# Attention probabilities turned by VectorE and DMA instead of TensorE, values kept by token, in a six-layer local-attention stream

## Chip, cores and metric

One core of a Trainium2 chip runs the whole program. The metric is the device time in microseconds (us); the median of three runs of the kernel before is 1961.72 us (1958.45 to 1962.31).

## What is computed

The input is 2 sequences of 1024 tokens of width 128. A first phase (an RWKV-style recurrent layer, about the first 300 us, not touched by the change) is followed by six layers of local attention and a gated feed-forward. The part that the change touches, for each layer, with 16 heads of width 64 and windows of 32 tokens:

```python
qkv = x @ Wqkv;  q, k, v = split(qkv)            # 16 heads of 64
q, k = l2norm(q) * qs, l2norm(k) * ksc           # then rotary position, scaled
bk2, bv2 = look(bk), look(bv)                    # keys and values of this window of 32 and the one before
sim = einsum('bhwie,bhwje->bhwij', bq, bk2) * 8.0
attn = softmax(where(mask, -max, sim), -1)       # 32 queries x 64 keys, per window and head
out = einsum('bhwij,bhwje->bhwie', attn, bv2)
x = x + out @ Wo
x = x + (a * gelu(gate)) @ W2 + b2               # a, gate = layernorm(x) @ W1 + b1
```

## The kernel before

The stream phase treats 96 blocks of 128 tokens (16 blocks a layer, six layers) as one software pipeline. `stream(turn)` calls, for each engine, its own function `turn` once a block number n; inside it `at(lag, stage)` runs a stage for block n - lag, and `pair(lag, stage)` one for a pair of blocks, only in odd or only in even turns. The order within an engine is the order of the lines of its `turn`; nothing reorders it. Engines meet through counting semaphores: `X.after(n)` is the count once stage X has finished block n.

A block's way, with its lag: project q, k (four PSUM banks, `project_qk`) and v (`project_v`); VectorE multiplies by the rotary tables (`rotate`, three instructions a bank), ScalarE squares for the norms (`square`), VectorE sums them (`norms`); GpSimd adds the turned half (`add_turned`) and scales by the inverse norms (`unit`), all at lag 0 and 1. At lag 2 TensorE turns k and q (`turn_k`, `turn_q`), ScalarE reads them out, TensorE makes the scores (`scores`), VectorE takes the peaks and subtracts them, ScalarE takes the exponent (`exponent`), VectorE sums and inverts (`totals`), GpSimd scales (`unit_probs`). At lag 3 TensorE turns the probabilities (`turn_p`, eight 128x128 transposes into banks 6 and 7), ScalarE copies them out (`read_p`) into `p_T`, and TensorE makes the outputs (`outputs`, 64 small products of 64 rows by 64 columns by 32). These need the values of two windows as rows, which SyncE's queue places with 16 DMAs of 64 KB a block (`place_v`, into `v_win`). Lags 4 to 6 hold, for pairs of blocks: output projection (`project_o`), residual (`add_attention`), centring product (`centres`), variance, and the feed-forward.

Two turns make a pair: in the even turn TensorE has in addition the variances and the first gate products, in the odd turn the rest of the feed-forward, the output projection and, last, `centres`. I call the even turn **A** and the odd one **B**; a pair as measured here runs from one `centres` to the next. GpSimd's turn begins with `table_gains`, which makes the rotary tables that `rotate` of the same block waits for.

## Time and profile before

| what | value |
|---|---|
| median of 3 runs | 1961.72 us |
| profiled execution: its own time | 1961.85 us |
| its span in the trace | 1960.1 us |
| mean granted TensorE clock | 0.968 |
| busy, whole span: PE / DVE / ACT / POOL | 1809.8 / 1488.0 / 1241.2 / 1234.4 us |
| PE matmuls of `turn_p` | 768 (8 a block) |
| DMAs `v_win<-v_tok` | 1536 of 64.0 KB (16 a block) |

PE is TensorE's matmuls, PEld its weight loads, DVE VectorE, ACT ScalarE, POOL GpSimd, SP the queue of SyncE. Instructions that read at once as "x4" are merged; their durations overlap with the next row's start, because ends are modelled, so distances from start to start are what adds up. TensorE's records come in two for each fp32 product and in one for each transpose.

### The profile page before, as it was taken

What the parts mean: (1) busy time and instruction counts of PE and PEld (TensorE: products, weight loads), DVE (VectorE), ACT (ScalarE), POOL (GpSimd) and SP (SyncE); (2) the same over time, 40 slices, a digit from 0 to 9 for tenths busy, and PEclk for the clock granted to TensorE, in tenths of its full rate; (3) what the DMA queues carried; (4) which work ended last, traced back from release to release, by engine and by line L of the source; (5) the groups of instructions that cost most, each with busy time, mean ns of one, the idle gap of its engine ahead of it and who ended that gap; (6) DMA issues with size and microseconds to landing.
All of it is one profiled execution on the core that took longest, in us unless ns stands there. A gap on an engine that the chain in (4) does not pass through costs nothing.

```text
span 1960.1 us, 75595 instructions
## 1 busy us (share of the span) xinstructions
PE 1809.8 (92%) x31926; PEld 1253.5 (64%) x31926; DVE 1488.0 (76%) x2822; ACT 1241.2 (63%) x2413; POOL 1234.4 (63%) x789
## 2 busy tenths in 40 slices
PE   7477876999999999999999999999999999999995
PEld 2144453667667667777777767677767776666773
DVE  6699947878777778787878777787878787777763
ACT  6523214577676767676767676767676767677662
POOL 3466733766666666666666666666666666666650
PEclk9799967999999999999999999999999999999996
DMA  4444002222222242222423222422224222222220
GB/s 100 123 53 56 17 3 83 63 67 67 67 66 62 68 117 71 64 72 60 122 70 73 63 67 61 125 61 72 62 70 121 70 64 69 65 67 67 66 69 22
DMA packets 89777, 137.48 MB, mean 70 GB/s; under 512 B 27168, under 2 KB 32736, under 8 KB 88416
## 3 DMA queue, kind: packets, MB, share of 16 engines
q1 hardware_dynamic: 89440, 132.66, 28.2%
q8 instruction: 252, 4.13, 0.9%
q14 instruction: 85, 0.70, 0.1%
HBM read 29.79 MB, written 2.10 MB: 16 GB/s over the span
## 4 chain that ended last, share of the span: by engine, by line
PE 49%; DVE 14%; issue 8%; POOL 6%; ACT 6%; DVEq 0%; SPq 0%; ACTq 0%; POOLq 0%; DMA 0%
PE bank L1435 8%; PE bank L1342 8%; PE bank L1417 7%; PE bank L1355 7%; PE bank L1390 5%; DVE turnedhalf L1762 5%; PE bank L1347 5%; PE bank L1452 4%; PE bank L1476 3%; POOL probs L1304 3%; DVE qk L1758 2%; POOL qk L1280 2%; DVE rnorm L1768 2%; ACT q_T L1604 1%; DVE probs L1781 1%
## 5 line engine op out<-in xcount | busy, mean ns | idle before, releaser
L1286 POOL TENSOR_TENSOR qk<-qk,rnorm 128x1024 f32<-128x1024 f32 x192 | 361.4, 1903 | 366.0 <-ACT rnorm L1592 275.4
L1280 POOL TENSOR_TENSOR qk<-qk,turnedhalf 128x1024 f32<-128x1024 f32 x192 | 454.7, 2368 | 138.8 <-DVE turnedhalf L1762 138.8
L1758 DVE TENSOR_TENSOR qk<-bank,gains 128x512 f32<-128x512 f32 x384 | 262.8, 684 | 222.0 <-ACT squares L1582 207.8
L1342 PE MATMUL bank<-wqkv,x 128*128 128x512 f32 x768 | 378.1, 596 | 4.7 <-DVE v_tok L1738 2.9
L1582 ACT ACTIVATE squares<-bank 128x512 f32<-128x512 f32 x384 | 232.6, 606 | 153.4 <-PE bank L1342 150.6
L1762 DVE TENSOR_TENSOR turnedhalf<-bank,gains 128x256 f32<-128x256 f32 x768 | 286.3, 414 | 0.0
L1629 ACT ACTIVATE o_T<-bank 128x512 f32<-128x512 f32 x192 | 104.2, 598 | 229.5 <-PE bank L1417 229.5
L1768 DVE TENSOR_REDUCE rnorm<-squares 128x16 f32<-128x1024 f32 x192 | 230.8, 1202 | 2.8
L1417 PEld LDWEIGHTS bank<-p_T,v_win 64*64 64x64 f32 x12288 | 189.9, 135 | 60.2 <-issue 57.6
L1355 PEld LDWEIGHTS bank<-st_ident,qk 128*128 128x128 f32 x1536 | 178.6, 142 | 57.1 <-issue 50.9
L1347 PE MATMUL bank<-wqkv,x 128*128 128x512 f32 x384 | 202.5, 609 | 7.0 <-DVE turnedhalf L1762 6.9
L1417 PE MATMUL bank<-p_T,v_win 64*64 64x32 f32 x12288 | 201.6, 220 | 8.0 <-issue 5.6
L1355 PE MATMUL bank<-st_ident,qk 128*128 128x128 f32 x1536 | 192.7, 274 | 0.0
L1304 POOL TENSOR_TENSOR probs<-probs,total 128x1024 f32<-128x1024 f32 x96 | 182.9, 1905 | 13.5 <-DVE total L1790 13.5
L1342 PEld LDWEIGHTS bank<-wqkv,x 128*128 128x128 f32 x768 | 138.6, 191 | 68.4 <-issue 55.1
L1435 PE MATMUL bank<-o_T,wo 128*128 128x256 f32 x768 | 173.8, 379 | 0.0
L1435 PEld LDWEIGHTS bank<-o_T,wo 128*128 128x128 f32 x768 | 145.8, 190 | 39.4 <-issue 22.0
L1452 PE MATMUL bank<-xn_T,w 128*128 128x256 f32 (+1 forms) x576 | 163.5, 393 | 7.7 <-ACT gate_T L1655 1.5
L1390 PE MATMUL bank<-k_T,q_T 64*32 64x64 f32 x12288 | 156.6, 225 | 12.8 <-issue 11.3
L1390 PEld LDWEIGHTS bank<-k_T,q_T 64*32 64x32 f32 x12288 | 136.6, 105 | 37.7 <-issue 34.0
L1808 DVE SCALAR_TENSOR_TENSOR ff_T<-bank,b,gate_T 128x256 f32<-128x256 f32 x144 | 64.7, 477 | 117.2 <-PE bank L1452 117.2
L1622 ACT ACTIVATE p_T<-bank 128x512 f32<-128x512 f32 x192 | 104.3, 594 | 75.5 <-PE bank L1355 74.4
(197 smaller groups left out, 2946.9 us busy)
## 6 DMA issues: line engine op xcount, KB each, us to landing
v_win<-v_tok SPq DMA_DIRECT2D x1536, 64.0 KB
wqkv<-in_wqkv SPq DMA_DIRECT2D x6, 1536.0 KB
v_rep_sb<-v_by_step SPq DMA_DIRECT2D x32, 128.0 KB
v_rep<-v_by_step SPq DMA_DIRECT2D x32, 128.0 KB
wo<-in_wo SPq DMA_DIRECT2D x6, 512.0 KB
w<-in_w SPq DMA_DIRECT2D x6, 341.0 KB
w<-in_w SPq DMA_DIRECT2D x6, 192.0 KB
xT_sb<-in_xT SPq DMA_DIRECT2D x1, 1024.0 KB, 4.9
```

Of the source, the lines that this page charges most:

```text
L1280: nc.gpsimd.tensor_tensor(out=qk[n % 2][:, half], in0=qk[n % 2][:, half], in1=turnedhalf[:, half], op=ALU.add).then_inc(rot_added.sem, 1)
L1286: nc.gpsimd.tensor_tensor(out=by_head(qk[u][:, half]), in0=by_head(qk[u][:, half]), in1=rnorm[u][:, AH * i:AH * (i + 1)].unsqueeze(2).to_b ...
L1342: nc.tensor.matmul(QK_BANKS[i][:, :], shifted_tokens(x, n, P), layer_cols(wqkv, n, 3 * INNER, 512 * i, 512), start=True, stop=True).then_i ...
L1347: nc.tensor.matmul(V_BANKS[i][:, :], shifted_tokens(x, n, P), layer_cols(wqkv, n, 3 * INNER, 2 * INNER + 512 * i, 512), start=True, stop=T ...
L1355: mm = nc.tensor.transpose(outs[i // 4][:, P * (i % 4):P * (i % 4 + 1)], source[:, P * i:P * (i + 1)], ident[:, :])
L1390: mm = nc.tensor.matmul(s_banks(n)[p][at:at + WINDOW, 2 * WINDOW * a_:2 * WINDOW * (a_ + 1)], q_T[rows, a_, at:at + WINDOW], k_T[rows, a_, ...
L1417: mm = nc.tensor.matmul(s_banks(n)[p][DH * side:DH * (side + 1), P * q + at:P * q + at + WINDOW], v_win[n % 2][rows, w, DH * a_:DH * (a_ + ...
L1435: mm = nc.tensor.matmul(ff_bank(m)[:, 0:PT], layer_cols(wo, n, INNER, C * i, C), o_T[:, i, :], start=(i == 0), stop=(i == PAIRS - 1))
L1452: mm = nc.tensor.matmul(ff_bank(m)[0:size, PT * j:PT * (j + 1)], layer_cols(w1, PAIR * m, 2 * FF, at + f0, size), xn_T[:, :], start=True, ...
L1758: nc.vector.tensor_tensor(by_head(qk[u][:, cols]), src, cos.to_broadcast([P, 8, DH]), ALU.mult).then_inc(rotated.sem, 1)
L1762: nc.vector.tensor_tensor(by_head(turnedhalf[:, cols])[:, :, to], src[:, :, frm], sin[:, :, to].to_broadcast([P, 8, half]), ALU.mult).then ...
L1768: nc.vector.reduce_sum(rnorm[n % 2][:, AH * h:AH * (h + 1)], by_head(squares[:, INNER * h:INNER * (h + 1)]), AX).then_inc(ss_made.sem, 1)
```

## The change

1. Probabilities: TensorE's eight transposes and ScalarE's two copies a block go. One VectorE instruction turns all 32x32 pieces of a block's probabilities into `p_blocks` (new `turn_p`, first in VectorE's turn), and eight DMAs of 32 partitions by 2 KB bring them to the rows where `outputs` reads them (new `place_p`, into two buffers `p_T`). In SyncE's queue the probabilities of block n - 2 (LAG_P = 2) go ahead of the values of block n.
2. Values: ScalarE writes them by token as they come (`read_v`, four buffers instead of three). `outputs` takes half its windows straight from `v_tok`, and the others from `v_shift`, the same shifted by 32 tokens, which two DMAs a block fill in place of 16. The same 64 products a block now run in another order: two column halves of the same rows, then two of the other rows.
3. Outputs are written to the scores' banks as before, with rows and columns laid out by window pair; `read_o` and the host's layout of Wo follow. `turn_k` waits only for the last block's copies.
4. Order: `totals` ahead of the last `rotate` on VectorE, `unit_probs` ahead of the second `add_turned` on GpSimd, `project_qk(2)` right behind the scores on TensorE. The end of the program is ordered anew.

```diff
-    v_win = two("v_win", (P, WINDOWS, INNER // 2))
-    probs, p_T = two("probs", (P, PAIRS, 2, DH)), sb("p_T", (P, PAIRS, P))
+    v_shift = two("v_shift", (P, INNER))
+    probs, p_T = two("probs", (P, PAIRS, 2, DH)), two("p_T", (P, 2, AH, WINDOW))
+    p_blocks = sb("p_blocks", (P, 2, AH, WINDOW))
...
         def place_v(n):
             sp.wait_ge(v_read.sem, v_read.after(n))
             sp.wait_ge(o_product.sem, o_product.after(n - 2))
             sp.wait_ge(v_placed.sem, v_placed.after(n - 1))
-            for p in range(2):
-                cols = slice(p * INNER // 2, (p + 1) * INNER // 2)
-                for w in range(WINDOWS):
-                    own, before = slice(WINDOW * w, WINDOW * (w + 1)), slice(WINDOW * (w - 1), WINDOW * w)
-                    sp.dma_start(v_win[u][DH * p + WINDOW:DH * (p + 1), w, :], tok[own, cols]).then_inc(v_placed.sem, 16)
-                    src = tok[before, cols] if w else last[P - WINDOW:P, cols]
-                    sp.dma_start(v_win[u][DH * p:DH * p + WINDOW, w, :], src).then_inc(v_placed.sem, 16)
+            sp.dma_start(v_shift[u][WINDOW:P, :], tok[0:P - WINDOW, :]).then_inc(v_placed.sem, 16)
+            sp.dma_start(v_shift[u][0:WINDOW, :], last[P - WINDOW:P, :]).then_inc(v_placed.sem, 16)
+        def place_p(n):
+            sp.wait_ge(p_turned.sem, p_turned.after(n))
+            sp.wait_ge(o_product.sem, o_product.after(n - 2))
+            sp.wait_ge(p_placed.sem, p_placed.after(n - 1))
+            for w in range(WINDOWS):
+                for half in range(2):
+                    row = DH * (w // 2) + WINDOW * half
+                    sp.dma_start(p_T[n % 2][row:row + WINDOW, w % 2, :, :], p_blocks[WINDOW * w:WINDOW * (w + 1), half, :, :]).then_inc(p_placed.sem, 16)
+        def place(n):
+            if n >= LAG_P:
+                place_p(n - LAG_P)
+            place_v(n)
...
         def outputs(n, q):
             if q == 0:
-                pe.wait_ge(pT_made.sem, pT_made.after(n))
...
+                pe.wait_ge(v_read.sem, v_read.after(n))
                 pe.wait_ge(v_placed.sem, v_placed.after(n))
+                pe.wait_ge(p_placed.sem, p_placed.after(n))
-            for w in range(WINDOWS):
-                for side in range(2):
-                    for p in range(2):
+            for a_ in (2 * q, 2 * q + 1):
+                for turn_ in range(2):
+                    v = v_tok[n % V_SLOTS] if turn_ else v_shift[n % 2]
+                    for g in range(2):
+                        for p in range(2):
+                            rows, head = slice(DH * g, DH * (g + 1)), 2 * a_ + p
+                            at = DH * a_ + WINDOW * turn_
+                            mm = nc.tensor.matmul(o_banks(n)[g][DH * p:DH * (p + 1), at:at + WINDOW], v[rows, DH * head:DH * (head + 1)],
+                                                  p_T[n % 2][rows, turn_, head, :], start=True, stop=True, skip_group_check=True)
...
+        def turn_p(n):
+            dve.wait_ge(p_normed.sem, p_normed.after(n))
+            dve.wait_ge(p_placed.sem, p_placed.after(n - 1))
+            nc.vector.transpose(p_blocks[:, :, :, :], probs[n % 2][:, :, :, :].rearrange("t a p (g k) -> t g (a p) k", k=WINDOW)).then_inc(p_turned.sem, 1)
```

On VectorE, in turn A and up to the start of turn B, there stood before (L1758 and L1762 are `rotate`, L1788 and L1790 `totals`, L1768 `norms`, L1808 `gated_full`):

```order
L1768 TENSOR_REDUCE rnorm<-squares 128x16
L1758 TENSOR_TENSOR qk<-bank,gains 128x512
L1762 TENSOR_TENSOR turnedhalf<-bank,gains 128x8x32 x2
L1758 TENSOR_TENSOR qk<-bank,gains 128x512
L1762 TENSOR_TENSOR turnedhalf<-bank,gains 128x8x32 x2
L1788 TENSOR_REDUCE total<-probs 128x16
L1790 RECIPROCAL total<-total 128x16
L1768 TENSOR_REDUCE rnorm<-squares 128x16
L1808 SCALAR_TENSOR_TENSOR ff_T<-bank,b,gate_T 128x256 x2
```

and at the same place there now stands (the line numbers of the changed kernel: L1764 and L1768 `rotate`, L1794 and L1796 `totals`, L1774 `norms`, L1802 the new `turn_p`, L1820 `gated_full`):

```order
L1774 TENSOR_REDUCE rnorm<-squares 128x16
L1764 TENSOR_TENSOR qk<-bank,gains 128x512
L1768 TENSOR_TENSOR turnedhalf<-bank,gains 128x8x32 x2
L1794 TENSOR_REDUCE total<-probs 128x16
L1796 RECIPROCAL total<-total 128x16
L1764 TENSOR_TENSOR qk<-bank,gains 128x512
L1768 TENSOR_TENSOR turnedhalf<-bank,gains 128x8x32 x2
L1774 TENSOR_REDUCE rnorm<-squares 128x16
L1802 STREAM_TRANSPOSE p_blocks<-probs 128x1024
L1820 SCALAR_TENSOR_TENSOR ff_T<-bank,b,gate_T 128x256 x2
```

The sums moved ahead of the last rotation, and the block transpose came in behind the norms' sum.

On GpSimd, from one `table_gains` (L1273) to the next, there stood before (L1286 `unit`, L1280 `add_turned`, L1304 `unit_probs`, L1298 or L1296 the halo of k):

```order
L1273 TENSOR_TENSOR gains<-tables,qk_gain 128x256
L1286 TENSOR_TENSOR qk<-qk,rnorm 128x1024 x2
L1280 TENSOR_TENSOR qk<-qk,turnedhalf 128x1024 x2
L1304 TENSOR_TENSOR probs<-probs,total 128x1024
L1273 TENSOR_TENSOR gains<-tables,qk_gain 128x256
```

and now stands (L1296 is now `table_gains`, L1309 `unit`, L1303 `add_turned`, L1327 `unit_probs`, L1319 the halo):

```order
L1296 TENSOR_TENSOR gains<-tables,qk_gain 128x256
L1309 TENSOR_TENSOR qk<-qk,rnorm 128x1024 x2
L1303 TENSOR_TENSOR qk<-qk,turnedhalf 128x1024
L1327 TENSOR_TENSOR probs<-probs,total 128x1024
L1303 TENSOR_TENSOR qk<-qk,turnedhalf 128x1024
```

The scaling of the probabilities moved between the two additions; all three still lie ahead of the next block's tables.

## Rows read from the trace of the kernel before

**Rows 1.** Busy time by engine in one steady pair (instruction counts, granted clock, DMA share, GB/s).

```profile
1023.35:1055.83 32.48, 32.37 (x627) 23.19 (x628) 25.73 (x49) 23.34 (x45) 22.39 (x14) 1.00 0.28 67
```

**Rows 2.** PE timeline, same pair: start us, us, engine line op, tiles, count.

```profile
1023.20 0.70 PE L1442 MATMUL bank<-xm,centring 128*128 128x256 f32 x2
...
1034.89 2.07 PE L1417 MATMUL bank<-p_T,v_win 64*64 64x32 f32 x128
1036.89 1.13 PE L1347 MATMUL bank<-wqkv,x 128*128 128x512 f32 x2
...
1042.88 0.66 PE L1452 MATMUL bank<-xn_T,w 128*85 128x256 f32 x2
...
1045.33 1.09 PE L1355 MATMUL bank<-st_ident,probs 128*128 128x128 f32 x8
1046.26 1.46 PE L1476 MATMUL bank<-ff_T,w 128*128 128x256 f32 x6
...
1055.68 0.70 PE L1442 MATMUL bank<-xm,centring 128*128 128x256 f32 x2
```

**Rows 3.** DVE timeline, same pair: brackets give idle time before and releaser.

```profile
1028.37 0.69 DVE L1758 TENSOR_TENSOR qk<-bank,gains 128x512 f32<-128x512 f32 x1 [4.34 <-ACT squares L1582]
...
1036.00 0.68 DVE L1758 TENSOR_TENSOR qk<-bank,gains 128x512 f32<-128x512 f32 x1
...
1037.27 1.21 DVE L1788 TENSOR_REDUCE total<-probs 128x16 f32<-128x1024 f32 x1
1038.51 0.25 DVE L1790 RECIPROCAL total<-total 128x16 f32<-128x16 f32 x1
1038.68 1.16 DVE L1768 TENSOR_REDUCE rnorm<-squares 128x16 f32<-128x1024 f32 x1
1041.95 0.88 DVE L1808 SCALAR_TENSOR_TENSOR ff_T<-bank,b,gate_T 128x256 f32<-128x256 f32 x2 [2.11 <-PE bank L1452]
1042.75 0.68 DVE L1758 TENSOR_TENSOR qk<-bank,gains 128x512 f32<-128x512 f32 x1
...
1054.43 0.82 DVE L1795 TENSOR_TENSOR xm<-bank,x 64x256 f32<-64x256 f32 x2
```

**Rows 4.** POOL timeline, same pair.

```profile
1037.43 2.37 POOL L1280 TENSOR_TENSOR qk<-qk,turnedhalf 128x1024 f32<-128x1024 f32 x1 [0.81 <-DVE turnedhalf L1762]
1039.76 1.90 POOL L1304 TENSOR_TENSOR probs<-probs,total 128x1024 f32<-128x1024 f32 x1
1041.62 0.74 POOL L1273 TENSOR_TENSOR gains<-tables,qk_gain 128x256 f32<-128x256 f32 x1
```

**Rows 5.** First and last centring product of the steady stretch, PE timeline (46 pairs).

```profile
393.55 1.22 PE L1442 MATMUL bank<-xm,centring 128*128 128x256 f32 x2 [1.60 <-DVE xm L1795]
...
1883.55 0.70 PE L1442 MATMUL bank<-xm,centring 128*128 128x256 f32 x2
```

**Rows 6.** PE timeline of a longer pair, 661.5 to 695.3.

```profile
676.13 0.32 PE L1417 MATMUL bank<-p_T,v_win 64*64 64x32 f32 x7 [1.02 <-issue]
```

**Rows 7.** DVE groups by line and shape, 0 to 320 us: the only block transpose.

```profile
L725 DVE STREAM_TRANSPOSE v_rep_sb<-decay 128x256 f32<-128x256 f32 x8 | 3.0, 419 | 0.0
```

**Rows 8.** Chain of waits, 1000 to 1060: start us, us, what.

```profile
1047.72 1.72 PE bank L1342 x4
...
1050.30 3.45 PE bank L1435 x16
1053.75 2.04 PE bank L1417 x128
```

**Rows 9.** SP timeline: the last placement of a block.

```profile
1046.84 0.59 SPq L1231 DMA_DIRECT2D v_win<-v_tok  x1
```

**Rows 10.** DMA busy tenths, 40 slices, 1045 to 1050 us.

```profile
DMA  0485105952010049510496104691000000000000
```

**Rows 11.** DMA rate, 40 slices, 969 to 989 us, after a layer's weights are issued.

```profile
GB/s 74 127 131 221 74 270 418 393 467 393 418 418 320 393 380 319 229 286 312 264 404 206 205 206 252 209 119 82 37 152 115 70 98 33 0 0 0 0 0 0
```

**Rows 12.** PE timeline of the end: outputs of the last block.

```profile
1913.65 2.07 PE L1417 MATMUL bank<-p_T,v_win 64*64 64x32 f32 x128 [2.20 <-ACT p_T L1622]
```

98 lines of the change are left out of this document (44 added, 54 removed).

## Prediction

> **What bounds the kernel now.** I first read the busy time of one steady pair. TensorE is busy 32.37 of 32.48 us, VectorE 25.73, ScalarE 23.34, GpSimd 22.39, at full granted clock [rows 1]. So TensorE sets the pace of a pair: from one centring product to the next, 1055.68 - 1023.20 = 32.48 us [rows 2]. Second, the timelines of the other engines over the same pair, for how far behind that pace they are. VectorE has two gaps a pair: 4.34 us ahead of turn A's first rotation, until ScalarE's squares come, and 2.11 us ahead of turn B's gated product, until TensorE has made it [rows 3]. They look like ample room, but a loop runs beside TensorE that is almost as long: first rotation of A at 1028.37; its last ends when GpSimd's addition starts, 1037.43; GpSimd then works without a gap, addition, probabilities, tables, until 1041.62 + 0.74 = 1042.36; turn B's first rotation, which waits for those tables, starts at 1042.75; the residual ends at 1054.43 + 0.82 = 1055.25; the centring product starts at 1055.68 [rows 2 to 4]. Of the 32.48 us this loop has 0.39 + 0.43 us of slack. That is what the change can win before something else is the bound.
>
> Third, all pairs: 46 centring products from 393.55 to 1883.55, so 45 pairs of 33.11 us on average [rows 5]. The 0.63 us above 32.48, 28 us in all, are mostly stops like the one of [rows 6]: TensorE waits 1.02 us in the middle of a train of small products, for nothing that the trace shows.
>
> **The change, part by part.** The sum is made per pair, then times 45, plus the ends.
>
> *TensorE.* Turn_p takes 1046.26 - 1045.33 = 0.93 us from start to start [rows 2], twice a pair: -1.86 us of TensorE, so its own work is 30.62 us. ScalarE's two copies a block go too; ScalarE is not short of time, and nothing in the loop waits for them.
>
> *Outputs.* 64 products of the same shape. Their order goes from alternating row halves to two column halves of the same rows at a time. The trace has 2.04 us for the 128 records [rows 8], 16 ns each, and no train in the new order. Lower bound: no change. Upper bound: twice as slow, 4 us, if two products on the same rows no longer overlap. I take no change: the weights of a full-array product seem to cost nothing although they go to the rows that are in use. Four records of 512 columns take 1.72 us, 430 ns each; sixteen of 256 columns take 3.45 us, 216 ns each [rows 8], so the time follows the columns and no fixed part for a weight load is left.
>
> The Trainium skill says the contrary of this reading: TensorE: Matmul & The Clock Gate, The mechanism, has weight loads overlap running products only where the row group differs. By it the new order, with pairs on the same rows, would be slower than the old. The trace of before agrees with it in the small products only so far that they alternate rows; in the full-array products it disagrees. What it would do here is the second rival.
>
> *VectorE.* One block transpose of 128x1024 a block. The trace has one of 128x256, 419 ns [rows 7]; four times that is 1.68 us, and as a single sweep like the sum of 128x1024 it is 1.21 us [rows 3]. In A it follows the norms' sum, which ends at 1038.68 + 1.16 = 1039.84. Even with 1.68 it ends at 1041.52, ahead of the 1041.95 at which the gated product can start. In B it falls into the gap of 4.34 us. I cost it at nothing; it would start to cost beyond 1.8 us, since the two gated products (0.80 us from 1041.95 to 1042.75) must then be done by the 1042.50 at which the tables come, below.
>
> *The reordering, on the loop.* The last rotation used to start at 1036.00 in A. Now the sums start there and their inverse is ready 1038.51 + 0.25 - 1037.27 = 1.49 us later, 1037.49. The handover to GpSimd, 0.08 us, gives 1037.57. Then GpSimd has the same three instructions as before in another order, 1.86 + 2.33 + 0.74 us (start to start) [rows 4], until 1042.50, and turn B's first rotation follows at 1042.56. Before, it started at 1042.75, held by the gated products; those are now 0.9 us earlier with TensorE. So this half gains 0.19 us.
>
> *Turn B.* From its first rotation to the end of the residual VectorE has 1055.25 - 1042.75 = 12.50 us without a wait on TensorE [rows 3], with the same instructions in another order. The residual now ends at 1055.06, and the centring product starts at 1055.12 in place of 1055.68. TensorE, 1.86 us of work shorter, is there before and waits more than 1 us. From the centring product to A's first rotation it is 5.17 us (1023.20 to 1028.37) as before, through TensorE's v and k products and ScalarE. So a pair takes 32.48 - 0.56 = 31.92 us, and 45 pairs save 25 us.
>
> *The stops.* In B TensorE now has 1.3 us to spare before it holds the loop (1.86 less the 0.56 gained), in A about half a us. A stop of 1 us costs its full length now; half of them should disappear in that room: -14 us, between 0 and -28.
>
> *SyncE's queue.* A block's probabilities need eight issues of 1047.43 - 1046.84 = 0.59 us [rows 9], 0.63 us apart, 5.05 us, and the last placement's packets are gone by 1048.4, 1.0 us after its issue [rows 9, 10]. In A, the tighter turn, counted from the centring product: the norms' sum ends at +1.1, the transpose at +2.8 at the latest, the issues at +7.8, the data at +8.9. The outputs start at 1034.89 - 1023.20 - 0.93 = +10.76 [rows 2]. So 1.8 us are left, and the transfers are hidden. The values' two DMAs are issued when the outputs of the block two before are done, ahead of the probabilities of the next, and do not queue behind them. If that cover goes, TensorE waits in `outputs`, and the k and q of the next turn, the gated product and the loop wait behind it.
>
> *Layer loads.* Four times, 2.7 MB of weights are issued directly behind the values, and now directly ahead of a block's probabilities. The transfer of those weights runs at some 400 GB/s and has died down after about 15 us, the v placements among them [rows 11]; 2.7 MB at 370 GB/s are 7.3 us. Probabilities queued behind them land at about +10 to +12 against +10.76. I take +1 us each, +4, between 0 and +12.
>
> *The end.* The last block's outputs start at 1913.65, released by ScalarE's copy [rows 12]. There the path of the probabilities lies open: 1.2 to 1.7 + 5.05 + 1.0 us in place of 0.93 and about 1.1 us. That is +5 us, less what TensorE no longer does there: +4, between 0 and +8.
>
> Sum: -25 - 14 + 4 + 4 = -31 us against the profiled execution's 1961.85 us, which stands 0.1 us from the median of the runs. Forecast: **1931 us**.
>
> **Rivals.** (a) *TensorE stays the bound*, since the loop is shorter than I read it: the pair falls to 30.6 us, 45 x 1.86 = 84 us less, 1878 us. For it: TensorE has nearly no gap now. Against: the GpSimd chain has none either, from 1037.43 to 1042.36.
>
> (b) *Outputs in the new order are slow.* Place: every `outputs`. At 4 us instead of 2.04, TensorE's pair is 30.62 + 4 = 34.6 us, 2.1 us more than now, 45 x 2.1 = +95 us and the ends: 2060 us, slower. It decides against the change from 2.04 + 0.93 = 3.0 us per block. At 2.7 us it costs almost nothing, in the room that TensorE has won. The skill's rule, above, points here.
>
> (c) *Probabilities come late in every turn.* If an issue takes 0.9 instead of 0.63 us, or a landing 3 us instead of 1, `outputs` of A starts some 0.5 to 1 us late; the gain of 0.56 is used up once the lateness goes beyond about 2.4 us. Then about 1965 us, slower or the same.
>
> (d) *Nothing changes*: the transpose takes over 2.4 us, or the loop grows elsewhere by what it gains, 1958 to 1964 us.
>
> **How the numbers follow.** My forecast (faster by 5 to 57 us, 1905 to 1957): 0.66. (a) 0.07, (b) 0.10, (c) 0.08, (d) 0.09. The forecast's own range comes from the bounds: -25 - 28 = -53, or 1909, and -25 + 12 + 8 = -5, or 1957. For 8 in 10 I take in (d) and half of (c): 1900 to 1965. A measurement here tells about 0.2%, 4 us, from no change. Faster 0.73 (forecast and (a)), same 0.10, slower 0.17 ((b) and most of (c)).
>
> **What would show it.** In the profile after: pairs of 31.9 us between centring products; TensorE busy about 30.6 us in each, and waiting over 1 us at the centring product for VectorE's residual; turn B's first rotation released by GpSimd's tables; the block transpose between 1.2 and 1.7 us, in both turns without a product waiting on it; a train of outputs of 2.0 us; TensorE waiting for no DMA in `outputs` but at four layer starts and at the end. I am wrong if the train of outputs is much longer, if its start is released by a DMA in ordinary turns, or if the pair is 30.6 us.

## The result, and the profile after

The changed kernel takes 1952.92 us (median of 20 runs, 1944.96 to 1959.65) where the kernel before takes 1963.18 us (20 runs on the same chips, 1955.27 to 1968.52). The ratio is 0.9949, with a 95% interval of 0.9937 to 0.9962: faster by 0.5%, about 10 us. I had forecast 31 us. The direction is right and the time lies inside the range, but the forecast is three times too large, and the reason for that is most of what follows. That the time lies inside the range is in part luck: one term missed its own bounds by far, and others, larger than forecast the other way, made up for some of it.

The page of the profiled execution after, its busy times and the DMA queue of instructions:

```profile
span 1954.8 us, 73483 instructions
...
PE 1766.6 (90%) x31158; PEld 1188.3 (61%) x31158; DVE 1598.5 (82%) x2918; ACT 1138.5 (58%) x2221; POOL 1233.5 (63%) x789
...
q8 instruction: 246, 4.03, 0.9%
```

TensorE is 43 us less busy, VectorE 111 us more (a block transpose of 1.24 us a block is 119 us of it). The span is only 5.3 us shorter: this execution took 1956.77 us, 4 us more than the median of its kernel, and the one profiled before 1.3 us less than the median of its own. What follows takes these two spans apart, not the 10 us of the medians.

One steady pair, its busy times (the stretch that answers to [rows 1]), and the two centring products that bound it, with the outputs of its second turn between them:

```profile
1022.02:1053.80 31.78, 31.33 (x611) 21.61 (x611) 28.00 (x51) 21.16 (x42) 22.35 (x14) 1.00 0.26 69
```

```profile
1021.96 0.70 PE L1462 MATMUL bank<-xm,centring 128*128 128x256 f32 x2 [0.26 <-DVE xm L1807]
...
1051.44 0.32 PE L1438 MATMUL bank<-p_T,v_shift 64*64 64x32 f32 x8
...
1053.76 0.70 PE L1462 MATMUL bank<-xm,centring 128*128 128x256 f32 x2 [0.26 <-DVE xm L1807]
```

A pair takes 1053.76 - 1021.96 = 31.80 us, where it took 32.48 [rows 2]; most pairs of the stretch take 31.78 to 31.80, and I use 31.79. The bracket is the new thing: at 40 of the 46 centring products TensorE now waits for VectorE's residual, where it did at one of 46 before. VectorE in the pair before that one:

```profile
1002.99 1.22 DVE L1794 TENSOR_REDUCE total<-probs 128x16 f32<-128x1024 f32 x1
...
1006.74 1.24 DVE L1802 STREAM_TRANSPOSE p_blocks<-probs 128x1024 f32<-128x1024 f32 x1
1008.20 0.88 DVE L1820 SCALAR_TENSOR_TENSOR ff_T<-bank,b,gate_T 128x256 f32<-128x256 f32 x2 [0.22 <-PE bank L1472]
1009.57 0.69 DVE L1764 TENSOR_TENSOR qk<-bank,gains 128x512 f32<-128x512 f32 x1 [0.50 <-issue]
...
1021.04 0.87 DVE L1807 TENSOR_TENSOR xm<-bank,x 64x256 f32<-64x256 f32 x2
...
1027.13 0.69 DVE L1764 TENSOR_TENSOR qk<-bank,gains 128x512 f32<-128x512 f32 x1 [2.82 <-ACT squares L1598]
```

And GpSimd in the same stretch, which answers to [rows 4]:

```profile
1004.57 1.90 POOL L1327 TENSOR_TENSOR probs<-probs,total 128x1024 f32<-128x1024 f32 x1 [0.97 <-DVE total L1796]
1006.43 2.36 POOL L1303 TENSOR_TENSOR qk<-qk,turnedhalf 128x1024 f32<-128x1024 f32 x1
1008.75 0.73 POOL L1296 TENSOR_TENSOR gains<-tables,qk_gain 128x256 f32<-128x256 f32 x1
```

This is the loop as the prediction has it: the sums, then GpSimd's probabilities, addition and tables without a gap until 1009.48, then turn B's first rotation at 1009.57, for which VectorE stood 0.50 us. The row names no releaser, but GpSimd's tables, for which this rotation waits, end 0.09 us before it.

All pairs together, first and last centring product, for [rows 5]:

```profile
397.61 0.70 PE L1462 MATMUL bank<-xm,centring 128*128 128x256 f32 x2 [1.60 <-DVE xm L1807]
...
1868.11 0.70 PE L1462 MATMUL bank<-xm,centring 128*128 128x256 f32 x2
```

45 pairs in 1470.5 us, where they took 1490.0: 19.5 us less. With the pair at 31.79 and 32.48 us, the difference of the two spans is made up of five terms:

| term | before | after | difference |
|---|---|---|---|
| 45 pairs at the steady length | 1461.6 | 1430.6 | -31.0 us |
| excess of the four pairs at layer loads | 4.2 | 31.5 | +27.3 |
| excess of the other pairs (stops) | 24.2 | 8.4 | -15.8 |
| start to first centring product | 393.6 | 397.6 | +4.1 |
| last of these products to the end | 76.6 | 86.7 | +10.1 |
| span | 1960.1 | 1954.8 | -5.3 |

So most of the gain was given back at four places, and more of it at the two ends. Pairs at the loads took 40.57, 38.34, 41.69 and 38.05 us (34.00, 32.68, 34.82 and 32.57 before). SyncE's queue at the first of them, and TensorE there (all rows of `outputs` but the first are left out):

```profile
689.25 0.53 SPq L1213 DMA_DIRECT2D wqkv<-in_wqkv  x1
689.82 0.44 SPq L1213 DMA_DIRECT2D wo<-in_wo  x1
690.30 1.03 SPq L1213 DMA_DIRECT2D w<-in_w  x2
691.38 1.30 SPq L1214 DMA_DIRECT2D qk_gain<-in_qk_gain  x1
692.80 5.00 SPq L1243 DMA_DIRECT2D p_T<-p_blocks  x8
```

```profile
697.68 1.02 PE L1370 MATMUL bank<-wqkv,x 128*128 128x512 f32 x2
704.25 0.44 PE L1438 MATMUL bank<-p_T,v_shift 64*64 64x32 f32 x8 [5.55 <-DMA p_T<-p_blocks]
...
707.82 2.07 PE L1370 MATMUL bank<-wqkv,x 128*128 128x512 f32 x2
```

The placements of the probabilities are issued behind 2.7 MB of weights, and `outputs` waits 5.55 us for them (7.24 us at the third load). Then the loss goes on: the train of 128 records takes 707.8 - 704.2 = 3.6 us, not 2.04, since the granted clock stands at 0.50, the lower of TensorE's two levels (1.2 and 2.4 GHz), from 704.2 to 708.0, as the windows show:

```profile
697.00:702.00 5.00, 1.70 (x4) 0.40 (x3) 4.96 (x9) 3.66 (x5) 4.20 (x3) 1.00 0.87 232
704.20:708.00 3.80, 3.75 (x129) 3.71 (x130) 1.39 (x2) 0.00 (x0) 2.90 (x2) 0.50 0.02 4
708.00:716.00 8.00, 8.00 (x28) 5.10 (x28) 0.81 (x3) 6.13 (x11) 0.00 (x0) 0.72 0.49 131
```

(After the times: busy of PE, PEld, DVE, ACT and POOL, then granted clock, DMA share and GB/s.) TensorE stood idle from 698.7 to 704.2. The granted clock was still 1.00 until 702.0 and is 0.50 from 702.5 on, so it fell within the wait, and it stayed there until 712.

At the second and fourth load it looks otherwise. TensorE stops in the middle of the scores, and nothing in the trace releases it:

```profile
957.55 1.48 PE L1413 MATMUL bank<-k_T,q_T 64*32 64x64 f32 x120
962.61 0.44 PE L1413 MATMUL bank<-k_T,q_T 64*32 64x64 f32 x8 [3.59 <-issue]
```

`outputs`, which comes behind, does not wait for the probabilities there. The stop is not the whole cost of 6.5 us here either: the granted clock is 1.00 from 959.0 to 961.6 and 0.50 behind it.

```profile
961.80:968.40 6.60, 5.79 (x17) 3.20 (x18) 4.87 (x8) 0.60 (x1) 3.43 (x2) 0.50 0.60 156
```

### The profile page after: what moved, and what is told of

The parts are those of the page before. It is cut to its first block, busy times and chain, and to the rows that moved or that the text cites. A ratio compares the mean times of both kernels' runs of the same rounds, so it can differ in the third digit from the quotient of the medians.

```text
span 1954.8 us, 73483 instructions
## 1 busy us (share of the span) xinstructions
PE 1766.6 (90%) x31158; PEld 1188.3 (61%) x31158; DVE 1598.5 (82%) x2918; ACT 1138.5 (58%) x2221; POOL 1233.5 (63%) x789
## 4 chain that ended last, share of the span: by engine, by line
PE 31%; DVE 22%; issue 9%; POOL 9%; DMA 6%; ACT 3%; SPq 2%; DVEq 0%; ACTq 0%; POOLq 0%
PE bank L1455 7%; DVE turnedhalf L1768 6%; DMA v_shift<-v_tok 5%; POOL qk L1303 5%; PE bank L1438 5%; PE bank L1365 5%; PE bank L1413 4%; DVE qk L1764 3%; DVE total L1794 3%; DVE rnorm L1774 3%; PE bank L1496 3%; PE bank L1370 3%; POOL probs L1327 2%; PE bank L1472 2%; DVE probs L1787 2%
## 5 line engine op out<-in xcount | busy, mean ns | idle before, releaser
L1309 POOL TENSOR_TENSOR qk<-qk,rnorm 128x1024 f32<-128x1024 f32 x192 | 361.0, 1901 | 316.4 <-ACT rnorm L1608 310.9
L1303 POOL TENSOR_TENSOR qk<-qk,turnedhalf 128x1024 f32<-128x1024 f32 x192 | 454.4, 2367 | 7.5 <-DVE turnedhalf L1768 7.5
L1365 PE MATMUL bank<-wqkv,x 128*128 128x512 f32 x768 | 406.5, 614 | 8.0 <-issue 3.0
L1764 DVE TENSOR_TENSOR qk<-bank,gains 128x512 f32<-128x512 f32 x384 | 258.1, 672 | 159.1 <-ACT squares L1598 138.6
L1327 POOL TENSOR_TENSOR probs<-probs,total 128x1024 f32<-128x1024 f32 x96 | 182.7, 1903 | 180.6 <-DVE total L1796 180.6
L1768 DVE TENSOR_TENSOR turnedhalf<-bank,gains 128x256 f32<-128x256 f32 x768 | 286.2, 415 | 0.0
L1774 DVE TENSOR_REDUCE rnorm<-squares 128x16 f32<-128x1024 f32 x192 | 233.2, 1214 | 2.8
L1438 PEld LDWEIGHTS bank<-p_T,v_shift 64*64 64x64 f32 x6144 | 168.9, 138 | 75.1 <-issue 46.2
L1438 PE MATMUL bank<-p_T,v_shift 64*64 64x32 f32 x6144 | 194.1, 223 | 22.3 <-DMA p_T<-p_blocks 17.1
L1370 PE MATMUL bank<-wqkv,x 128*128 128x512 f32 x384 | 205.0, 616 | 4.7 <-DVE turnedhalf L1768 4.2
L1438 PE MATMUL bank<-p_T,v_tok 64*64 64x32 f32 x6144 | 192.8, 222 | 3.7 <-issue 3.7
L1413 PE MATMUL bank<-k_T,q_T 64*32 64x64 f32 x12288 | 164.0, 225 | 16.9 <-issue 15.7
L1438 PEld LDWEIGHTS bank<-p_T,v_tok 64*64 64x64 f32 x6144 | 170.0, 138 | 4.4 <-issue 4.4
L1413 PEld LDWEIGHTS bank<-k_T,q_T 64*32 64x32 f32 x12288 | 141.6, 105 | 45.4 <-issue 38.8
L1472 PEld LDWEIGHTS bank<-xn_T,w 128*128 128x128 f32 (+1 forms) x576 | 99.2, 184 | 101.2 <-DVE ff_T L1820 45.9
```

The source lines that it names most:

```text
L1303: nc.gpsimd.tensor_tensor(out=qk[n % 2][:, half], in0=qk[n % 2][:, half], in1=turnedhalf[:, half], op=ALU.add).then_inc(rot_added.sem, 1)
L1309: nc.gpsimd.tensor_tensor(out=by_head(qk[u][:, half]), in0=by_head(qk[u][:, half]), in1=rnorm[u][:, AH * i:AH * (i + 1)].unsqueeze(2).to_b ...
L1365: nc.tensor.matmul(QK_BANKS[i][:, :], shifted_tokens(x, n, P), layer_cols(wqkv, n, 3 * INNER, 512 * i, 512), start=True, stop=True).then_i ...
L1370: nc.tensor.matmul(V_BANKS[i][:, :], shifted_tokens(x, n, P), layer_cols(wqkv, n, 3 * INNER, 2 * INNER + 512 * i, 512), start=True, stop=T ...
L1413: mm = nc.tensor.matmul(s_banks(n)[p][at:at + WINDOW, 2 * WINDOW * a_:2 * WINDOW * (a_ + 1)], q_T[rows, a_, at:at + WINDOW], k_T[rows, a_, ...
L1438: mm = nc.tensor.matmul(o_banks(n)[g][DH * p:DH * (p + 1), at:at + WINDOW], v[rows, DH * head:DH * (head + 1)], p_T[n % 2][rows, turn_, he ...
```

## Experiments

Ratios are to the kernel before, timed beside each; the changed kernel has 0.9949. Each experiment starts from the changed kernel unless the text says otherwise.

### e1: the load behind the placements

```diff
+            place_p(layer * BLOCKS + EARLY - LAG_P)
...
             load_layer(sp, layer + 1, (layer + 1) % 2)
-            for n in range(EARLY, BLOCKS):
+            place_v(layer * BLOCKS + EARLY)
+            for n in range(EARLY + 1, BLOCKS):
                 place(layer * BLOCKS + n)
```

> The changed kernel with one edit: at each of the four layer loads inside the stream, SyncE issues the eight placements of the waiting block's turned probabilities before the five transfers of the next layer's weights, not behind them. In the changed kernel the four pairs at the loads take 40.6, 38.3, 41.7 and 38.1 us against 31.8 us for the others, +31.5 us in all. Theory A (the probabilities queue behind the weights, and outputs waits for them): the four pairs fall to at most 34 us each, so 22 to 31 us come back and the median is about 1926 us (1921 to 1932). Theory B (the weights fill the DMA engines, and TensorE stops for its own instructions whatever the order of the issues is): only the two loads at which outputs waited for the probabilities gain, about half of it, 1936 to 1943 us; the two loads at which TensorE stopped for 3.5 to 3.8 us inside the scores keep their stops.

Measured: 1931.73 us, ratio 0.982 (0.9797 to 0.9843), 25 us faster than the changed kernel by the ratios. SyncE now issues the placements at 687.65, the weights at 692.70:

```profile
687.65 4.95 SPq L1243 DMA_DIRECT2D p_T<-p_blocks  x8
692.70 1.10 SPq L1213 DMA_DIRECT2D wqkv<-in_wqkv  x1
```

The pairs at the first and third load are now 31.77 and 31.78 us, so all of their excess is gone. The other two hardly changed, 38.18 and 37.76 us; the second one:

```profile
940.21 0.70 PE L1464 MATMUL bank<-xm,centring 128*128 128x256 f32 x2 [0.26 <-DVE xm L1809]
...
956.86 0.31 PE L1440 MATMUL bank<-p_T,v_tok 64*64 64x32 f32 x2 [2.92 <-issue]
...
978.39 0.70 PE L1464 MATMUL bank<-xm,centring 128*128 128x256 f32 x2 [0.25 <-DVE xm L1809]
```

So in places theory B is right: two loads gain and two keep stops. This pair has two, 0.90 and 2.92 us; the first ends at 948.23, ahead of the weights, which are issued at 948.72. Its time, 1936 to 1943 us, was too high, because the two waits for the probabilities were worth 19 us and not half of 31.5, and some further microseconds came from elsewhere.

### e4: the load in parts

```diff
+    LOAD_PARTS = [("wqkv", c, c + 512) for c in range(0, 3 * INNER, 512)] + ...
...
-            load_layer(sp, layer + 1, (layer + 1) % 2)
             for n in range(EARLY, BLOCKS):
                 place(layer * BLOCKS + n)
+                i = n - EARLY
+                if i == 0:
+                    load_gain(sp, layer + 1, (layer + 1) % 2)
+                for part in range(2 * i, min(2 * i + 2, len(LOAD_PARTS))):
+                    load_part(sp, layer + 1, (layer + 1) % 2, part)
```

> The changed kernel with one edit: each of the four layer loads inside the stream is cut into eleven parts of at most 256 KB, of which SyncE issues two behind the placements of each block, from the block on at which the whole load was issued before. Theory A (order behind the weights): the probabilities never wait for more than two parts, so the loads' +31.5 us fall to a few us: about 1926 us. Theory B (the DMA engines are full during a load, and TensorE's own instructions come late): as the engines are never full for longer than 1 to 2 us, its stops of 3.5 to 3.8 us go as well, and this kernel is faster than the one that only moves the load behind the probabilities: 1920 to 1930 us here, against 1936 to 1943 there. If both come out alike within 3 us, TensorE's stops at the loads cost nothing of their own. Against both: each part costs SyncE about 0.63 us of issuing, eleven instead of four, which could make the placements later by 1.3 us a block; then the blocks of the load lose up to 6 x 1.3 = 8 us a layer.

Measured: 1923.09 us, ratio 0.9782 (0.976 to 0.9804). The pair at the second load is 972.12 - 939.82 = 32.30 us:

```profile
939.82 0.70 PE L1477 MATMUL bank<-xm,centring 128*128 128x256 f32 x2 [0.25 <-DVE xm L1822]
...
972.12 0.70 PE L1477 MATMUL bank<-xm,centring 128*128 128x256 f32 x2 [0.25 <-DVE xm L1822]
```

No pair at a load is longer than 32.6 us, and no train of the steady stretch is stopped for more than 1.5 us. The four loads are now all but free, and against e1 8.6 us came back (the intervals of the ratios just touch; timed together, all five runs of e4 are faster than all four of e1). So the long stops came with the whole load in the engines at once, and the twelve issues in place of five cost SyncE nothing that shows in the time.

### e2: the order of sums and probabilities undone

```diff
-            at(2, totals)
             at(0, rotate, 3)
+            at(2, totals)
...
-            at(2, unit_probs)
             at(0, add_turned, 1)
+            at(2, unit_probs)
```

> The changed kernel with the two moves in order undone: on VectorE the sums of the exponentials stand behind the last rotation of the bank again, and on GpSimd the product that makes unit probabilities stands behind both additions of the rotation. The instructions are the same. Theory A (a loop through VectorE and GpSimd sets the pair: rotation, sums, unit probabilities, additions, next rotation, residual, centring product): the unit probabilities and with them the placements come later, and the loop is longer by what was moved out of it; pair 33.0 us in place of 31.8, +54 us, about 2005 us. Theory B (TensorE sets the pair with its stops and trains, and the others have room): within 0.3% of the changed kernel, 1948 to 1958 us.

Measured: 2003.88 us, ratio 1.0194 (1.0167 to 1.0221). The pair is 1075.28 - 1042.48 = 32.80 us, 1.0 us more than in the changed kernel, and the order on GpSimd shows why: its addition waits for the last rotation, and the tables end at 1028.85, after which turn B begins.

```profile
1023.92 2.37 POOL L1303 TENSOR_TENSOR qk<-qk,turnedhalf 128x1024 f32<-128x1024 f32 x1 [0.81 <-DVE turnedhalf L1768]
1026.24 1.90 POOL L1327 TENSOR_TENSOR probs<-probs,total 128x1024 f32<-128x1024 f32 x1
1028.11 0.74 POOL L1296 TENSOR_TENSOR gains<-tables,qk_gain 128x256 f32<-128x256 f32 x1
```

Theory A holds, with 1.0 us where I had 1.2. It also says what the rest of the change is worth without these two moves: the kernel is 1.9% slower than before. VectorE's block transpose then waits 1.85 us for GpSimd's probabilities and holds turn B's rotations, which start at 1030.10, 1.25 us after the tables.

### e3 and b1: the tables earlier, in both kernels

```diff
         def turn(at, pair):
             at(2, halo)
-            at(0, table_gains)
             at(1, unit, 0)
             at(1, unit, 1)
+            at(-1, table_gains)
...
+        table_gains(0)
```

> The changed kernel with GpSimd's product for the tables of the next block made right behind the two unit products of the block before, a turn's slack ahead of where it stands now (behind the unit probabilities and additions). The instructions are the same. Theory A (GpSimd's additions, tables and unit probabilities lie in the loop that sets the pair, and VectorE's second rotation of a pair waits for the tables): the loop is shorter by the part of the tables' 0.8 us that it now spends in it, pair 31.3 in place of 31.8 us, -22 us: 1931 us (1926 to 1940). Theory B (TensorE or VectorE alone sets the pair): no change, 1948 to 1958 us.

> The kernel before with GpSimd's product for the tables moved as in the run with early tables, nothing else. In the changed kernel this move took 0.35 us off each pair. The prediction held that the kernel before is bound by TensorE (pair 32.48 us), and the loop through VectorE and GpSimd bounds only the changed one. Theory A (so it is): no change, ratio 0.998 to 1.002, about 1965 us. Theory B (the loop already bounded the kernel before): pair 0.3 to 0.4 us shorter, 14 to 18 us, ratio 0.991 to 0.993.

Measured: e3 1943.54 us, ratio 0.988 (0.9858 to 0.9902); pair 1045.82 - 1014.39 = 31.43 us, 0.36 less. The tables are made at 1025.44, the two additions and the probabilities stand alone in the loop:

```profile
1025.44 0.74 POOL L1296 TENSOR_TENSOR gains<-tables,qk_gain 128x256 f32<-128x256 f32 x1
...
1028.77 1.91 POOL L1327 TENSOR_TENSOR probs<-probs,total 128x1024 f32<-128x1024 f32 x1 [0.27 <-DVE total L1797]
1030.64 2.36 POOL L1303 TENSOR_TENSOR qk<-qk,turnedhalf 128x1024 f32<-128x1024 f32 x1
```

The same edit in the kernel before (b1) gives 1962.9 us, ratio 0.9988 (0.9973 to 1.0004): nothing. So the first reading of the prediction holds on both sides. TensorE bounds the kernel before, and the loop through VectorE and GpSimd bounds the changed one. Of the 0.74 us of the tables only 0.36 us is gained, so something else holds the pair at 31.43 us. What it is I did not take apart; e8, below, shows that VectorE's order is still part of it.

### b2: the kernel before with its loads in parts

The edit of e4, in the kernel before.

> The kernel before with its layer loads cut into the same eleven parts, two behind the placements of each block. In its trace the pairs at the loads are no longer than the others. Theory A (the kernel before has nothing to gain there, so that the cost of the loads is one that the change brought): ratio 0.998 to 1.002, about 1965 us. Theory B (its stops of TensorE, 28 us over the stream, come partly from the loads): 0.995 to 0.998. Against both: its sixteen transfers a block take SyncE 10 us of the 16, and two more issues a block might make it late: then over 1.002.

Measured: 1962.25 us, ratio 0.9983 (0.9972 to 0.9995). That is 3 us, about the 4.2 us of excess that its pairs at the loads had, where the same edit brings 33 us in the changed kernel. The loads' cost came with the change, all but a small part. Two things are new. The probabilities stand behind the weights in SyncE's queue, which accounts for the first and third load (e1). And the weights are issued 1.1 to 1.6 us behind the centring product, in e1 7.4 to 8.5 us, where it was 10.9 to 11.6 us before, so they meet other work of TensorE. Whether that is why the kernel before has no long stop at its second and fourth load, no run tells.

### e7: the order of the outputs

```diff
-                for turn_ in range(2):
-                    v = v_tok[n % V_SLOTS] if turn_ else v_shift[n % 2]
-                    for g in range(2):
+                for g in range(2):
+                    for turn_ in range(2):
+                        v = v_tok[n % V_SLOTS] if turn_ else v_shift[n % 2]
```

> The changed kernel with its outputs' products in another order within each of the four parts of a train: the half of TensorE's rows (64 of 128) on which a product works changes every fourth product, where it changes every second in the changed kernel and every product in the kernel before. Theory A (the train's time is one issue of 16 ns per record, whatever the halves): 128 records in 2.04 us again, the same span as the changed kernel to 0.3%. Theory B, after the rule of the Trainium skill, page TensorE: Matmul & The Clock Gate, section The mechanism (a weight load hides behind running products only where its rows differ from theirs): three of four loads now stand in the same half, and the train takes longer than 2.04 us, by at least 10%.

Measured: one run, 1949.6 us, span 1947.7. The chain of waits has a steady train of the changed kernel, and below it one of e7:

```profile
1019.71 2.04 PE bank L1438 x128
```

```profile
1014.40 2.08 PE bank L1438 x128
```

The train of e7 is 2% longer, where theory B wants at least 10%, and the four pairs at the loads keep their excess (38.5 to 39.7 us), so the span, of a single run, is that of the changed kernel to 0.4%. With the row half changing every product (before, [rows 8]), every second (changed) or every fourth (e7), the train takes 2.04, 2.04 and 2.08 us. The rule of the Trainium skill, page TensorE: Matmul & The Clock Gate, section The mechanism, that a weight load overlaps running products only where its row group differs, is not seen in these trains of fp32 products of 32 columns; the measurement decides.

### e10: one and a half loads

e1, and behind each load one more transfer of 1.5 MB of weights into a spare buffer in DRAM that nothing reads.

> The kernel in which the layer load is issued behind the placements of the probabilities, with one more transfer behind each of the four loads: the 1.5 MB of the query, key and value weights are copied a second time, into a spare buffer in DRAM that nothing reads. No computation changes. Theory A (TensorE stops when its own instructions are fetched while the DMA engines are full; in the changed kernel a fetch of 16 KB came every 5 to 7 us, and at the second load none between 952.6 and 961.8 us while TensorE stood from 959.0 to 962.6): with the engines full for some 5 us longer at each load, stops of 2 us and more come at all four loads, not at two, and the time rises by 6 to 25 us over 1929 us. Theory B (the stops come from something at these places in the program and not from the transfers): they stay as they are at the second and fourth load, none come at the others, and the time stays within 3 us.

Measured: 1934.61 us, ratio 0.9847 (0.9817 to 0.9877), 5 us more than e1 by the ratios, within the two intervals. A stop came at the third load, whose pair is 35.04 us (31.78 in e1):

```profile
1227.28 0.48 PE L1503 MATMUL bank<-ff_T,w 85*128 85x256 f32 x1 [2.07 <-issue]
```

None came at the first, and the other two kept theirs, shorter than in e1 (36.19 and 36.48 us). Theory A expected all four and theory B none. This does not settle it: one more load has a stop, and the time did not move beyond the noise.

### e12: TensorE's instructions shifted

e1, and ahead of the stream 128 waits in place of one:

```diff
-        pe.wait_ge(masks_made.sem, 3)
+        for _ in range(128):
+            pe.wait_ge(masks_made.sem, 3)
```

> The kernel in which the layer load is issued behind the placements, with 128 further instructions ahead of TensorE's stream (waits on a semaphore that has long been set). In the trace the transfers of the instruction queue with 16 KB each come once for every 256 instructions of TensorE (246 of them for 31158 products, as many weight loads and 839 semaphore instructions), and against the pairs their times repeat every 5.5 pairs or so; as a layer has 8 pairs, the second and fourth load meet them half a cycle away from the first and third. Theory A (a fetch that falls into the time of a load comes late, and TensorE stops when it has run through what it has): 128 instructions are half a cycle, so the stops change places: the pairs at the first and third load now take 36 to 39 us, those at the second and fourth 31.8 to 33 us, and the time stays within 6 us of 1929. Theory B (the stops come from the place in the layer's program or from the load alone): second and fourth load take 38 us again, first and third 31.8.

Measured: 1930.11 us, ratio 0.9834 (0.9805 to 0.9863), as e1. The pair at the second load now has no excess at all, 978.08 - 946.30 = 31.78 us (38.18 in e1), nor has the one at the fourth (31.78 us; 37.76 in e1):

```profile
946.30 0.70 PE L1465 MATMUL bank<-xm,centring 128*128 128x256 f32 x2 [0.25 <-DVE xm L1810]
...
978.08 0.70 PE L1465 MATMUL bank<-xm,centring 128*128 128x256 f32 x2 [0.26 <-DVE xm L1810]
```

The pairs at the first and third load are 33.63 and 33.29 us (31.77 and 31.78 in e1), the third with a stop in the transposes:

```profile
1218.72 0.33 PE L1381 MATMUL bank<-st_ident,qk 128*128 128x128 f32 x1 [1.76 <-issue]
```

The long stops left the second and fourth load, as theory A says and theory B excludes: nothing but the position of TensorE's instructions against the loads was changed. That they came to the first and third is less clear. The excess there is 1.5 to 1.9 us in place of the 4 to 7 expected, and in the same run the pair ahead of the first load, in which no weights move, takes 34.04 us. One difference shows: the granted clock stays at 1.00 over both loads here (700 to 740 and 1210 to 1230 us), while it is 0.50 from 956.0 to 962.7 in e1. The whole kernel is not faster for it by more than its interval.

The transfers of the instruction queue bear theory A out. In the profile of the changed kernel that queue has 246 transfers (q8, above) for 31158 products, as many weight loads and 839 semaphore instructions: 63155 / 246 = 257 instructions each. Around the stop at the second load, the DMA queues from 951.6 to 960.2 us:

```profile
DMA packets 366, 2.35 MB, mean 273 GB/s; under 512 B 45, under 2 KB 45, under 8 KB 240
q1 hardware_dynamic: 366, 2.35, 79.7%
```

and from 960.2 to 960.4 us:

```profile
q1 hardware_dynamic: 14, 0.05, 98.3%
q8 instruction: 1, 0.02, 28.8%
```

The instruction transfer before these begins between 950.5 and 951.0 us. So there is none for 9.8 us while weights fill the engines. TensorE stands from 959.0 on, the transfer begins at 960.4, and TensorE goes on at 962.6. The distance of 9.8 us alone proves nothing: over the stream the transfers come every 6.7 us on average, half of them 5.2 to 8.3 us after the last, and in the kernel before two at its second load are 9.8 us apart without a stop. What ties the two together is the end of the stops. The one above ends 2.22 us after a transfer begins, the one at the fourth load 2.25 us, those of e1 2.26 and 2.27 us, that of e12 at the third load 2.21 us. The same holds of the ordinary stops: over the steady stretches of all sixteen profiles, the kernel before among them, TensorE stops 185 times for 0.7 us or more with nothing to release it, and every one of these stops ends 2.2 to 3.1 us after the beginning of an instruction transfer. Stops at random times would do so in about one case of seven. (The two times in the expectation of e10, 952.6 and 961.8, are 2.0 and 1.4 us too late: the transfers begin at 950.6 and 960.4.)

### e5, e6, e8, e9, e11: putting together what paid

e5 is e4 with the tables of e3. e6 adds two moves behind the stream's end, e9 the same with a weaker wait. e8 is e5 with one reduction moved on VectorE, e11 is e9 with that too:

```diff
 e6, e9 (VectorE)
-        add_attention(m - 1)
-        add_ffn(m - 2)
         turn_p(LAST)
+        add_attention(m - 1)
+        add_ffn(m - 2)
 e6, e9 (TensorE)
+        final_turn(0)
+        final_turn(1)
         attend(outputs, LAST)
         up_gate_full(m - 1)
-        final_turn(0)
-        final_turn(1)
 e9 only, in final_turn
-            pe.wait_ge(oT_made.sem, oT_made.after(LAST - 1))
+            pe.wait_ge(oT_made.sem, oT_made.after(LAST - 2))
 e8, e11 (VectorE)
-            at(0, norms, 0)
             at(0, rotate, 2)
             at(2, totals)
             at(0, rotate, 3)
             pair(4, add_attention)
+            at(0, norms, 0)
             at(0, norms, 1)
```

> The changed kernel with both edits that each paid alone: the layer loads cut into eleven parts behind the placements, and GpSimd's tables a turn's slack ahead. Alone, the first had a ratio to the kernel before of 0.978 and the second of 0.988, against 0.995 for the changed kernel with neither. Theory A (independent places: the loads at four pairs, the tables in every pair): the gains add, ratio about 0.971, 1908 us (1902 to 1914) where the kernel before takes 1965. Theory B (with the pair at 31.4 us instead of 31.8, another wait, for the squares from ScalarE or for the turned probabilities, sets the end of the pair): ratio 0.975 or more.

> The kernel with load parts and early tables, and two moves behind the stream's end: VectorE turns the last block's probabilities ahead of the residual and the sum of the two pairs before, and TensorE turns the first eight finished blocks (two groups of transposes) ahead of the last block's outputs, during the wait for its placement. In the changed kernel outputs of the last block waited 3.24 us for the placed probabilities at 1907.0, which VectorE began to turn at 1898.1 though they were there at 1894.7. Theory A (that placement is on the path to the end): the stretch from the last but one centring product on is 2 to 4 us shorter than in the kernel without the two moves, ratio 0.002 lower. Theory B (the end is set by the feed-forward products of the last two pairs, which come behind anyway): under 1 us.

> The kernel with load parts and early tables, and on VectorE the first of a block's two reductions of the squares (1.22 us) moved from ahead of the rotation's second half to behind it and behind the residual. Theory A (the loop through VectorE, totals, GpSimd and the residual's centring product still sets the pair of 31.45 us): the reduction leaves the way to totals and residual, and the pair becomes shorter by 0.3 to 1.2 us, ratio 0.955 to 0.968 to the kernel before. Theory B (at 31.45 us VectorE waits 2.8 us a pair for ScalarE's squares, so another chain already sets it, and the squares of the next block wait for this very reduction): same or slower, 0.972 to 0.985.

> The kernel with load parts, early tables and the two moves behind the stream's end again, but the first groups of final transposes no longer wait for ScalarE's read of the last but one block's outputs, only for that of the block before it, whose banks they take. In the run with the two moves that wait took 3.08 us on TensorE ahead of the last block's outputs. Theory A (it gave back what the moves brought): 3 us less than in that run, ratio 0.9705 to 0.9715. Theory B (the end is set by the feed-forward products behind): under 1 us less, ratio 0.972 to 0.973.

> All edits that paid together: layer loads in parts behind the placements, GpSimd's tables early, VectorE's first reduction of squares behind the residual, the last block's probabilities turned earlier, and the first final transposes ahead of the last outputs with the weaker wait. With the first three the ratio to the kernel before was 0.965 (pair 30.94 us), with the last two instead of the third 0.971 against 0.972. Theory A (the end's edits add to the loop's): 0.963 to 0.9645, 1893 us. Theory B (the end's gain was chance): 0.965 or more.

| kernel | us | ratio | interval | steady pair |
|---|---|---|---|---|
| e5 | 1910.48 | 0.9721 | 0.9702 to 0.974 | 31.46 |
| e6 | 1911.21 | 0.9725 | 0.9705 to 0.9744 | 31.46 |
| e9 | 1907.3 | 0.9709 | 0.9685 to 0.9733 | 31.46 |
| e8 | 1895.8 | 0.9648 | 0.9622 to 0.9674 | 30.94 |
| e11 | 1891.37 | 0.9625 | 0.96 to 0.9651 | 30.95 |

e5: the two gains add (theory A). e8: theory A again; the reduction leaves the way from the rotations to the residual, and the pair loses 0.52 us. That is less than half of the reduction's 1.22 us, because TensorE is the bound again: it is busy 30.79 of 30.90 us and waits at none of the 46 centring products. e6 brought nothing: its first transposes waited for ScalarE's read of the outputs ahead of the last ones,

```profile
1860.16 1.97 PE L1552 MATMUL bank<-st_ident,xf 128*128 128x128 f32 x8 [3.08 <-ACT o_T L1655]
```

and without that wait (e9) the stretch from the last centring product but two to the end is 1900.3 - 1821.5 = 78.8 us, in place of 83.8 in e5 and 89.1 in e6. But e11 ends in the same way as e9 and takes 83.5 us there. What differs is the granted clock: its mean over this stretch is 0.83 in e9, 0.74 in e11 and 0.73 in e5. The ratios say 2 to 3 us for e9, within the intervals, so the edits of the end are not shown to pay. e11, whose ratio is just below what theory A gave, has all of them and is 3.7% faster than the kernel before and 3.3% faster than the changed one.

## Why the prediction was right in its mechanism and wrong in its size

**The bound.** Right. TensorE bounded the kernel before (b1 finds nothing to win in GpSimd there), and the loop through sums, GpSimd and residual bounds the changed one (e2, e3 and e8 all move the pair the way they should: e2 lengthens it by 1.0 us where 1.2 was expected, e3 takes 0.36 of 0.74 us off it, e8 0.52 of 1.22, at which TensorE bounds it again).

**The pair.** 31.92 us forecast, 31.79 measured. -25 us forecast, -31 measured. The centring product waits for the residual, but 0.26 us and not over 1 us, and TensorE is busy 31.33 us and not 30.6. In e8, where the same products make a pair of 30.9 us, it is busy 30.79 us; so some 0.5 of the 31.33 us are waits that lie inside the busy times of pipelined products. That they make up the rest of the 1 us is my reading.

**Outputs, transpose, SyncE's queue.** Right. 2.04 us for the train, 1.24 us for the transpose, between my two bounds; no ordinary turn waits for the placements, whose eight issues take 4.95 us.

**The stops.** -14 forecast, -16 measured, of 24 us outside the loads. That the room took them up is argued, not shown by a run of its own. The reading "for nothing that the trace shows" was too weak: they end, as said under e12, 2.2 to 3.1 us after an instruction transfer begins.

**The layer loads.** This is the step that failed. I wrote: "Probabilities queued behind them land at about +10 to +12 against +10.76. I take +1 us each, +4, between 0 and +12." Measured: +27.3 us (31.5 of excess, where the kernel before had 4.2), beyond my upper bound. Three things were wrong in it. First, the last placement is issued at 697.80 - 687.80 = +10.0 already, since the five issues of the load stand ahead of the eight, and it then has to get through what the weights leave: `outputs` could start at 704.25, which is +16.5. I counted the time of the bytes but not the issues. Second, I took the wait to be the whole cost; the TensorE that stood for 5.55 us came back at half clock, which adds 1.6 us in the train and more behind it. Third, the two other loads cost 6.5 and 6.3 us without any wait for the probabilities to be seen in the trace. There TensorE stops for 3.59 and 3.29 us until 2.2 us after a late instruction transfer begins, and goes on at half clock. In [rows 11] the load ran at 400 GB/s, and I asked only what data would queue behind it. e1 and e4 give each its price: 19 us for the order (e1), and of the other 12.8 all but some 1.3 us for the whole load at once (e4).

**The end.** +4 forecast, between 0 and +8; +10.1 measured. The wait is there (3.24 us), and so is what I left out: a stop of 2.32 us ahead of it, during which the clock falls to 0.50; it stays there from 1900.5 to 1913.9.

```profile
1899.33 6.13 SPq L1243 DMA_DIRECT2D p_T<-p_blocks  x8
```

```profile
1901.13 0.32 PE L1438 MATMUL bank<-p_T,v_shift 64*64 64x32 f32 x2 [2.32 <-issue]
...
1907.02 0.44 PE L1438 MATMUL bank<-p_T,v_shift 64*64 64x32 f32 x8 [3.24 <-DMA p_T<-p_blocks]
```

There the eight issues also take 6.13 us, not the 5.05 by which I had counted. The size of this term is in part that of this one execution. In the ten profiles of kernels with the same end code (the changed one, e1 to e5, e7, e8, e10 and e12) the stretch takes 81.1 to 87.0 us, and it is the shorter the less of it runs at half clock: 51 us of it in the changed kernel's 86.7, 30.5 us in the 81.1 of e4. Against the 76.6 us of before that is +4.5 to +10.4. The +4.1 us ahead of the first centring product, for which the forecast has no term, vary too: e1, e2, e4, e7 and e10 have 394.3 to 397.9 us there.

**The rivals.** (a), TensorE still the bound at 30.6 us a pair, is refuted by the wait at the centring product and by e3. (b), slow outputs, is refuted by the train and e7. (c), late probabilities in every turn, did not come; `outputs` waited for them at the first and third load and at the end, at a price of its own. (d) is not it: the pair did get shorter.

## What to carry to other kernels

When a DMA is put into the path of a product, look at the worst turn and not at the usual one: what else is issued on that queue, in which order, and how many issues stand ahead. A load of weights that costs next to nothing today costs as soon as something urgent stands behind it; cutting it into parts and issuing them behind the urgent ones took away 33 us here, for twelve issues a layer in place of five. And a wait of TensorE of some microseconds is not priced by its length alone: look at the granted clock behind it.

Take the order of two engines' work as seriously as the work itself. With the turning moved off TensorE and the sums where they were, this kernel was 1.9% slower; with the sums one rotation earlier it became 0.5% faster, and with the loads, the tables and one reduction in their places 3.5% (e8).

## What the runs showed of the hardware that I had not expected

- TensorE's own instructions are a transfer of the same DMA engines: 246 transfers of 16 KB for 63155 instructions. During a whole load TensorE stood for up to 3.6 us in the middle of a train, and 127 more instructions ahead of the stream took the long stops away from the second and fourth load. All 185 stops of 0.7 us or more that nothing else releases, in sixteen profiles, end 2.2 to 3.1 us after such a transfer begins. That the transfer is what TensorE waits for is inferred from these two facts; why it is late at a load, and why some late ones bring no stop, is not shown.
- In a wait of 5.55 us TensorE's granted clock fell to 0.50, and it was 0.50 for the next 3.8 us and 0.72 on the average of the 8 us behind; the train of 128 records took 3.6 us in place of 2.04.
- A block transpose of 128x1024 fp32 on VectorE takes 1.24 us, where one of 128x256 takes 419 ns [rows 7]: about as long as a sum over the same tile (1.22 us), not four times the small one.
- The train of outputs does not depend on how often its products change the half of TensorE's rows: 2.04 us at every and at every second product, 2.08 us at every fourth.
